# Layers 3 and 4 of a coupling network as pairs of 64-wide tiles, with the layers of successive blocks interleaved

## The chip, the cores and the metric

The kernel runs on one core of a Trainium2 chip. The metric is the device time of one execution in microseconds. Five engines work side by side: TensorE (PE), VectorE (DVE), ScalarE (ACT), GpSimd (POOL) and SyncE (SP), which issues the transfers.

## What is computed

```python
x = x + layernorm(attention(layernorm(x)))           # x: (8, 512, 256)
x = x + layernorm(ffn(layernorm(x)))

def coupling_net(h):                                  # 256 -> 256 -> 128 -> 64 -> 1
    h = gelu(h @ w1 + b1)
    h = gelu(h @ w2 + b2)
    h = gelu(h @ w3 + b3)
    return sigmoid(h @ w4 + b4)

def ffn(x):
    gf = global_net(x.mean(axis=1, keepdims=True))    # 256 -> 128 -> 64 -> 1
    out = x
    for _ in range(3):
        combined = 0.7 * gf + 0.3 * coupling_net(out)
        coupling = 0.1 + adaptive_range * (combined - 0.5) * 2.0
        out = out + coupling * twist(out)             # twist permutes and negates quarters
    return out
```

The attention is a segmented one with a memory carried from segment to segment. The change does not touch it.

## The kernel before, in words

The attention takes the first 1075 us or so and works in four steps (segments of 128 rows) for each of four pairs of sequences. Its very end overlaps the start of the feed-forward part: the last segment's rows are still to be turned (`turn_att`, L1157), projected (`project_out`, L1172), normalised and added (`y_stats`, `y_norm`, `residual`, `x2_stats`, `x2_norm`) and turned once more (`turn_rows`, L1044), and these steps are written by hand between the first feed-forward stages.

The feed-forward part holds the activations transposed in SBUF (`XT`, features on partitions, float32). The 8 x 512 rows are four blocks `bb` (one for each pair of sequences), and a block is two halves `j` of 512 columns. There are three cycles over the four blocks, so twelve **stages**, here numbered m = 0 to 11; the code before counts halves, n = 2m. The four stages of cycle 2 (m = 4 to 7) are a hardware loop, the others are written out. A stage is `layers(n, bb)`:

- `layer1` (L1278): four results per stage, each of two matmuls (256 = 2 x 128 rows), 128x512, into four PSUM banks; ACT applies gelu to each (L636).
- `layer2` (L1291): two results, each of two matmuls, into two banks; gelu (L644).
- `layers34`: for each half one matmul of w3 (L1298), which gives 64 output partitions, always partitions 0 to 63, and a gelu over 64 partitions (L649); then for each half one matmul of w4 (L1301), which contracts these 64 rows and gives the same sum on all 128 partitions, and a tanh (L658).
- `update` on DVE: two TENSOR_SCALARs make the coupling from the tanh (L961), then L966, L967 and L969 the products and the sum for the first 128 features; POOL subtracts for the other 128 (L456).

A float32 matmul is two records of PE in the trace, and each has a weight load before it.

Every engine runs its own instruction list in order and waits on semaphores. The order of the work is written out by hand, once for each engine. `net(half, layer)` is the small global network: half 0 (the first three pairs) in stage 0, half 1 (the last pair) in stage 3, where it waits for `seq_sums` (L849, L861) on DVE. `couple` turns its result into the base of the coupling.

In cycle 3 each block is finished after its stage. `back(t)` (L1262) transposes a tile of 128x512 back into a PSUM bank, four tiles for each block; `f_stats` (L976, L979) and `f_shift` (L984) on DVE with `f_dev` (L461, L463) on POOL give the layer norm's scale and shift; ACT normalises into SBUF (L674); POOL adds the residual (L468; DVE adds the last two tiles, L997); SP stores a block in eight transfers (L346). DVE and POOL have `finish(bb - 1)` ahead of `update` of stage 8 + bb. `back` of a block stands on PE in the stage after it, between layer 2 and layer 3:

```python
layer1(n, bb, half, last - NSEG if last else None)
layer2(n)
if last is not None:
    ...
    for t in range(last, last + NSEG):
        ...
        back(t)
layers34(n)
```

## Time and profile before

| | |
|---|---|
| time, median of 3 runs | 1298.55 us (1297.96 to 1299.42) |
| profiled execution, span | 1296.2 us |
| what lies around the span, against that median | 2.4 us |
| PE busy | 1091.5 us (84%) |
| DVE busy | 913.4 us (70%) |
| ACT busy | 596.7 us (46%) |
| POOL busy | 582.6 us (45%) |

The profiled execution has no time of its own among the three, only its span; its own time is taken as the span and the 2.4 us around it, and so stands level with the median. The span is cut into stretches below: the attention up to about 1075 us, the feed-forward stages from there to 1269 us, and the rest. A timeline row gives the start in us from the span's start, the length, the engine, the line, what is written and read, the shape and the number of records; in square brackets stands the idle time of the engine before it and who ended it. PEclk is the granted TensorE clock as a share of 2.4 GHz (1.00 is 2.4 GHz, 0.50 is 1.2 GHz).

### The profile page before, as it was taken

To read this page: it belongs to the slowest core of one execution; us is meant where nothing else is said; L and a number is where in the kernel's file an instruction comes from. 1 tells how busy PE (TensorE), PEld (TensorE's weight loads), DVE (VectorE), ACT (ScalarE), POOL (GpSimd) and SP (SyncE) were. 2 spreads that over 40 slices of the span, in tenths; PEclk is the share of its full clock that TensorE was granted. 3 is DMA by queue.
4 is the path that set the end of the run, shared out by engine and by line. 5 is a ranking of instruction groups with operands and counts; after the bars stand their busy time and mean duration, and the time that the engine had idled before them with its cause. 6 is when DMAs were issued, how large, how long until landed. Compare 5 with 4: busy or idle time off the path is not lost.

```text
span 1296.2 us, 20762 instructions
## 1 busy us (share of the span) xinstructions
PE 1091.5 (84%) x7108; PEld 764.7 (59%) x7172; DVE 913.4 (70%) x1668; ACT 596.7 (46%) x1255; POOL 582.6 (45%) x715
## 2 busy tenths in 40 slices
PE   3798889886989898878888888798989779999992
PEld 1476657564767575647676756576767665433431
DVE  4868686876686868657878786868686754444486
ACT  4344444544454444443535354445444543444463
POOL 2145454544454545434545454545454552222274
PEclk9899999988899999989999999989999888999996
DMA  5000000000000000000000000000000010300033
GB/s 159 20 9 9 10 9 11 8 14 6 10 9 9 9 9 10 10 10 10 9 9 9 9 10 9 9 9 9 9 1 9 1 28 1 138 0 0 1 65 65
DMA packets 14681, 24.00 MB, mean 19 GB/s; under 512 B 5104, under 2 KB 6896, under 8 KB 14064
## 3 DMA queue, kind: packets, MB, share of 16 engines
q1 hardware_dynamic: 14576, 22.63, 5.7%
q8 instruction: 62, 1.02, 0.3%
q14 instruction: 43, 0.35, 0.1%
HBM read 13.97 MB, written 8.65 MB: 17 GB/s over the span
## 4 chain that ended last, share of the span: by engine, by line
PE 41%; DVE 38%; issue 11%; ACT 6%; POOL 2%; DMA 1%; DVEq 1%; SPq 0%; POOLq 0%; ACTq 0%
DVE arena L769 10%; PE ps L1172 9%; PE ps L1067 8%; PE ps L1278 6%; DVE arena L867 3%; PE ps L1125 3%; DVE arena L788 3%; ACT arena L555 3%; PE ps L1291 3%; DVE arena L819 2%; PE ps L1112 2%; DVE arena L713 2%; DVE arena L801 2%; DVE arena L779 2%; DVE arena L782 2%
## 5 line engine op out<-in xcount | busy, mean ns | idle before, releaser
L1067 PE MATMUL ps<-arena 128*128 128x512 f16 x1152 | 270.8, 386 | 6.0 <-DVE arena L745 4.2
L555 ACT ACTIVATE arena<-ps,arena 128x128 f32<-128x128 f32 x512 | 140.7, 381 | 252.4 <-DVE arena L791 251.3
L769 DVE STREAM_TRANSPOSE arena<-ps 128x1024 f32<-128x1024 f32 x96 | 189.8, 1979 | 35.4 <-PE ps L1067 35.4
L1067 PEld LDWEIGHTS ps<-arena 128*128 128x128 f16 x1152 | 113.1, 100 | 129.4 <-issue 14.0
L402 POOL TENSOR_TENSOR arena<-arena 128x256 f32<-128x256 f32 x128 | 93.1, 728 | 153.3 <-DVE arena L801 153.3
L1125 PEld LDWEIGHTS ps<-arena 128*128 128x128 f32 x1024 | 135.7, 202 | 29.5 <-issue 21.2
L1125 PE MATMUL ps<-arena 128*128 128x65 f32 x1024 | 139.2, 281 | 16.2 <-DVE arena L801 15.0
L386 POOL TENSOR_TENSOR arena<-arena 128x512 f32<-128x512 f32 x64 | 81.2, 1268 | 135.4 <-ACT arena L548 135.2
L1112 PE MATMUL ps<-arena 128*128 128x128 f32 x512 | 84.5, 303 | 45.6 <-ACT arena L555 45.5
L1172 PE MATMUL ps<-arena 128*128 128x256 f32 x544 | 122.0, 382 | 0.3 <-ACT arena L567 0.3
L372 POOL TENSOR_TENSOR arena<-arena 128x2 f32<-128x2 f32 x50 | 9.8, 196 | 230.8 <-DVE arena L709 230.8
L1172 PEld LDWEIGHTS ps<-arena 128*128 128x128 f32 x544 | 102.0, 190 | 16.0 <-issue 0.8
L705 DVE BATCH_NORM_STATS2 arena<-arena 128x6 f32<-128x256 f32 x100 | 36.7, 409 | 100.1 <-ACT arena L573 85.0
L1145 PE MATMUL ps<-arena 128*128 128x130 f32 x384 | 69.3, 320 | 42.6 <-DVE arena L730 24.1
L1112 PEld LDWEIGHTS ps<-arena 128*128 128x128 f32 x512 | 63.1, 154 | 65.1 <-ACT arena L555 64.5
L404 POOL TENSOR_TENSOR arena<-arena 128x256 f32<-128x256 f32 x128 | 93.1, 728 | 10.0
L406 POOL TENSOR_TENSOR arena<-arena 128x256 f32<-128x256 f32 x128 | 93.1, 727 | 10.0
L801 DVE TENSOR_TENSOR arena<-ps,arena 128x512 f32<-128x512 f32 x128 | 88.5, 692 | 12.4
L788 DVE TENSOR_REDUCE arena<-ps 128x4 f32<-128x512 f32 x128 | 87.0, 680 | 13.1 <-PE ps L1101 12.7
L561 ACT ACTIVATE arena<-ps 128x1024 f32<-128x1024 f32 x64 | 65.7, 1026 | 65.9 <-PE ps L1112 65.9
L713 DVE TENSOR_SCALAR arena<-arena 128x256 f32<-128x256 f32 x100 | 68.7, 728 | 36.5 <-POOL arena L374 36.5
L1130 PE MATMUL ps<-arena 128*128 128x130 f32 x512 | 91.0, 303 | 0.0
(110 smaller groups left out, 1920.9 us busy)
## 6 DMA issues: line engine op xcount, KB each, us to landing
x_rows<-arena SPq DMA_DIRECT2D x17, 256.0 KB, 2.0
arena<-in_L_attn_x_dram SPq DMA_DIRECT2D x64, 64.0 KB
arena<-x_rows SPq DMA_DIRECT2D x4, 1024.0 KB, 7.9
out_dram<-arena SPq DMA_DIRECT2D x32, 128.0 KB, 2.9
arena<-in_L_attn_Wq_dram SPq DMA_DIRECT2D x1, 1024.0 KB, 12.3
arena<-in_L_attn_Wk_dram SPq DMA_DIRECT2D x1, 1024.0 KB, 14.4
arena<-in_L_attn_Wv_dram SPq DMA_DIRECT2D x1, 1024.0 KB, 17.4
arena<-in_L_attn_Wo_dram SPq DMA_DIRECT2D x1, 1024.0 KB, 13.0
```

The lines of the kernel that those rows point to most:

```text
L402: pool.tensor_tensor(mem, mem, dot, ALU.subtract).then_inc(mix, 1)
L404: pool.tensor_tensor(mem, mem, gt, ALU.mult).then_inc(mix, 1)
L406: pool.tensor_tensor(att[:, u * DK:(u + 4) * DK].rearrange("p (u e) -> p u e", u=4), mem, dot, ALU.add).then_inc(att_done, 1)
L555: last = act.activation(Pr[:, par, j, :], s_bank[:, par, j * P:(j + 1) * P], ACT.Exp, scale=SCALE, bias=shift[:, par, j:j + 1])
L713: last = dve.tensor_scalar(dst[:, w * D:(w + 1) * D], src[:, w * D:(w + 1) * D], mv[:, w, 0:1], rs[:, w:w + 1], ALU.subtract, ALU.mult)
L769: dve.transpose(dst[:, d0:d0 + 32, :], bank.rearrange("p w (d c) -> p d w c", c=C)).then_inc(x_free, 1)
L788: dve.tensor_reduce(negm[:, par, :], s_bank[:, par, :].rearrange("p (j i) -> p j i", j=GP), AX.X, ALU.max, negate=True).then_inc(m_done, 1)
L801: dve.tensor_tensor(AB[half], rd[:, :, :, 0:DK], rr.rearrange("p m (u a) -> p m u a", a=1).to_broadcast([P, 2, 4, DK]), ALU.mult).then_inc ...
L1067: last = pe.matmul(bank[:, w, :], xc[:, lx, k, w * P:(w + 1) * P], W16[lw][:, k, i, :], start=(n == 0), stop=(n == 5))
L1112: last = pe.transpose(s_bank[:, par, j * P:(j + 1) * P], Pr[:, par, j, :], identf)
L1125: pe.matmul(pm_bank[:, 0, u * DV1:(u + 1) * DV1], PT[:, par, j, :], v[:, GU * g + 2 * j + par, 0:DV1], start=True, stop=True)
L1172: last = pe.matmul(t_bank[b][:, w * D:(w + 1) * D], attT[:, w, j, :], Wo_sb[:, j, :], start=(j == 0), stop=(j == 7))
```

## The change

`layer3` writes its second half to partitions 64 to 127 of the same bank, so both halves share one bank and one gelu over 128 partitions, and one semaphore step instead of two. In the built program the second matmul carries the array position (0, 64) in tiles of 128x64. `layer4` contracts partitions 0 to 63 for the first half and 64 to 127 for the second (array positions (0, 0) and (64, 0), tiles of 64x128), into two different banks, with one semaphore step. w4 and b3 are loaded a second time onto the upper partitions (two transfers more), and `h3` is one buffer.

A stage m now runs layer 1 of its first half, layer 3 of stage m - 1, layer 1 of its second half, layer 4 of stage m - 1, layer 2. Layer 4 of stage 0 stands after `project_out`. On DVE and POOL `update` of stage 0 moves behind `y_norm` and `residual`. In cycle 3 the finishes move one place back in each list and `back` moves out of the stages: block 0 is transposed after stage 10, block 1 after stage 11, blocks 2 and 3 after the last layer 4. New banks are given to layers 3 and 4 and to `back`, with waits on them: layer 1 of stage 11 and layer 4 of stage 10 now wait for the normalised tiles of block 0.

```diff
-        l3_bank = [l1_bank[0], l1_bank[2]]
-        back_bank = [ps[:, b, :] for b in (1, 5, 2, 3)]
+        l3_bank = l2_bank[0]
+        y_job = t_job(PAIRS - 1, NSEG, "Y")
+        pair_bank = t_bank[y_job[0]]
+        solo_bank = t_bank[1 - y_job[0]]
+        back_banks = [(l1_bank[2], l1_bank[3], solo_bank, pair_bank)] * 2 + [
+            tuple(l1_bank), (l2_bank[0], l2_bank[1], solo_bank, pair_bank)]
         net_job = [t_job(PAIRS - 1, NSEG, j) for j in ("A1", "F")]
+
+        def back_bank(t):
+
+            return back_banks[t // NSEG][t % NSEG]
+
+        def l4_bank(m, j):
+
+            return (l2_bank[1], l2_bank[0] if isinstance(m, int) and m in (0, LAST_M) else pair_bank)[j]
...
-                        (w3, cw3), (w4[0:64], cw4), (g1, gw1.rearrange("(k p) n -> p k n", k=KT)), (g2, gw2),
+                        (w3, cw3), (w4[0:64], cw4), (w4[64:P], cw4), (g1, gw1.rearrange("(k p) n -> p k n", k=KT)), (g2, gw2),
                         (g3[0:64], gw3), (b1, cb1.rearrange("(m p) -> p m", m=2)), (b2, col(cb2)),
-                        (b3[0:64], col(cb3)), (b4, col(cb4).to_broadcast([P, 1])), (c1, col(gb1)),
+                        (b3[0:64], col(cb3)), (b3[64:P], col(cb3)), (b4, col(cb4).to_broadcast([P, 1])), (c1, col(gb1)),
...
-                update(0, 0)
                 y_dev(PAIRS - 1, NSEG)
                 residual(PAIRS - 1, NSEG)
+                update(0, 0)
                 x2_dev(PAIRS - 1, NSEG)
...
+                update(2 * CYCLE_M, 0)
+                update(2 * CYCLE_M + 1, 1)
+                finish(0)
+                update(2 * CYCLE_M + 2, 2)
+                finish(1)
+                finish(2)
+                finish(3, 2)
...
+                def stage(m, prev=None, half=None, last=None):
+
+                    if half is not None:
+                        net(half, 0)
+                    layer1(m, 0)
+                    if last is not None:
+                        normalise(last)
+                    if prev is not None:
+                        layer3(prev)
+                    if last is not None:
+                        normalise(last + 1)
+                    if half is not None:
+                        net(half, 1)
+                    layer1(m, 1)
+                    if half is not None:
+                        net(half, 2)
+                    if last is not None:
+                        normalise(last + 2)
+                        normalise(last + 3)
+                    if prev is not None:
+                        layer4(prev)
+                    layer2(m)
...
+                layer3(0)
+                take_y(y_job)
+                layer4(0)
+                stage(1)
                 take_f(t_job(PAIRS - 1, NSEG, "F"), NT - 1)
-                layers(4)
-                layers(6, 1)
+                stage(2, 1)
+                stage(3, 2, 1)
...
-                update(0, 0)
                 y_stats(PAIRS - 1, NSEG)
                 y_norm(PAIRS - 1, NSEG)
+                update(0, 0)
                 x2_stats(PAIRS - 1, NSEG)
                 x2_norm(PAIRS - 1, NSEG)
-                update(2, 1)
+                update(1, 1)
                 seq_sums(PAIRS - 1, NSEG)
-                update(4, 2)
+                update(2, 2)
                 couple(1)
-                update(6, 3)
+                update(3, 3)
...
+                update(2 * CYCLE_M, 0)
+                update(2 * CYCLE_M + 1, 1)
+                finish(0)
+                update(2 * CYCLE_M + 2, 2)
+                finish(1)
+                update(LAST_M, 3, True)
+                finish(2)
+                finish(3)
...
+                def back(bb):
+
+                    for t in range(bb * NSEG, (bb + 1) * NSEG):
+                        done = (2 * CYCLE_M + bb) * 2 + t % NSEG // 2 + 1
+                        pe.wait_ge(up_a, done)
+                        pe.wait_ge(up_b, done)
+                        if bb == 3 and t % NSEG < 2:
+                            pe.wait_ge(th_done, 2 * LAST_M + 2)
+                        elif bb < 2 and t % NSEG == 3:
+                            pe.wait_ge(th_done, 2 * (2 * CYCLE_M + bb + 1) + 2)
+                        if t >= NSEG:
+                            pe.wait_ge(fn_done, 2 * (t - NSEG + 1))
+                        for w in range(2):
+                            for k in range(KT):
+                                last = pe.transpose(back_bank(t)[:, w * D + k * P:w * D + (k + 1) * P],
+                                                    XT[:, k, (2 * t + w + 2) * P:(2 * t + w + 3) * P], identf)
+                        last.then_inc(f_full, 1)
...
+                    for c in range(2):
+                        if last is not None and j == 1:
+                            pe.wait_ge(fn_done, 2 * (last + c + 1))
...
+                        pe.wait_ge(l1_act, m * 4 + 2 * (j + 1))
+                        if isinstance(m, int) and m == 1:
+                            pe.wait_ge(th_done, 2)
+                        elif j == 1 and not (isinstance(m, int) and m == 0):
+                            pe.wait_ge(th_done, m * 2 - 1)
+                        for k in range(2):
+                            done = pe.matmul(l2_bank[j], w2[:, k, :], h1[j][:, k, :],
+                                             start=(k == 0), stop=(k == 1))
+                        done.then_inc(l2_full, 1)
+
+                def layer3(m):
+                    pe.wait_ge(l2_act, m * 2 + 2)
+                    for j in range(2):
+                        done = pe.matmul(l3_bank[64 * j:64 * j + 64], w3, h2[j], start=True, stop=True)
+                    done.then_inc(l3_full, 1)
+
+                def layer4(m, last=None):
+                    pe.wait_ge(l3_act, m + 1)
+                    if isinstance(m, int) and m == 1:
+                        pe.wait_ge(t_free[y_job[0]], y_job[1] + 1)
+                    if not (isinstance(m, int) and m == 0):
+                        pe.wait_ge(th_done, m * 2)
+                    if last is not None:
+                        pe.wait_ge(fn_done, 2 * (last + NSEG))
+                    for j in range(2):
+                        p = slice(64 * j, 64 * j + 64)
+                        done = pe.matmul(l4_bank(m, j), w4r[p], h3[p], start=True, stop=True)
+                    done.then_inc(l4_full, 1)
+
...
+                    layer1(m, bb, 0)
+                    if prev is not None:
+                        layer3(prev)
+                    if half is not None:
+                        net(half, 1)
+                    layer1(m, bb, 1, last)
                     if half is not None:
+                    if prev is not None:
+                        layer4(prev, last)
+                    layer2(m)
...
-                layers34(0)
-                project_out(t_job(PAIRS - 1, NSEG, "Y"), [t_job(PAIRS - 1, NSEG, a) for a in ("A2", "A3")])
-                layers(2, 1)
+                layer3(0)
+                project_out(y_job, [t_job(PAIRS - 1, NSEG, a) for a in ("A2", "A3")])
+                layer4(0)
+                stage(1, 1)
                 turn_rows(t_job(PAIRS - 1, NSEG, "F"), row, x2n_done, NT + 1)
-                layers(4, 2)
+                stage(2, 2, 1)
                 pe.wait_ge(xt_done, NT + 1)
-                layers(6, 3, 1)
+                stage(3, 3, 2, 1)
...
+                    m = 2 * CYCLE_M + bb
+                    stage(m, bb, m - 1, None, 0 if bb == PAIRS - 1 else None)
+                    if bb >= 2:
+                        back(bb - 2)
+                layer3(LAST_M)
+                layer4(LAST_M)
+                back(PAIRS - 2)
+                back(PAIRS - 1)
```

The update function's counts change from n to 2m and are the same otherwise. (L1320, L1333, L1340, L1353 and L1307 of the new file are layers 1, 2, 3, 4 and `back`; L993 to L1001 the update.)

**PE, the end of the program**, from layer 1 of stage 11. Before:

```order
L1278 MATMUL ps<-arena 128x512 x8
L1291 MATMUL ps<-arena 128x512 x4
L1262 MATMUL ps<-arena 128x128 x16
L1298 MATMUL ps<-arena 64x512 x2
L1301 MATMUL ps<-arena 128x512 x2
```

and in the change, where the first L1307 is block 0's `back`, after stage 10:

```order
L1307 MATMUL ps<-arena 128x128 x16
L1320 MATMUL ps<-arena 128x512 x4
L1340 MATMUL ps<-arena 64x512 x2
L1320 MATMUL ps<-arena 128x512 x4
L1353 MATMUL ps<-arena 128x512 x2
L1333 MATMUL ps<-arena 128x512 x4
L1307 MATMUL ps<-arena 128x128 x16
L1340 MATMUL ps<-arena 64x512 x2
L1353 MATMUL ps<-arena 128x512 x2
L1307 MATMUL ps<-arena 128x128 x32
```

Layers 3 and 4 of a stage moved into the stage behind it, and two blocks are left to be transposed at the very end, where one was.

**DVE, the start of the feed-forward part.** Before, the update of stage 0 and then the two normalisations:

```order
L961 TENSOR_SCALAR arena<-arena 128x16x16 x2
L966 TENSOR_TENSOR arena<-arena 128x512
L967 TENSOR_TENSOR arena<-arena 128x512
L969 TENSOR_TENSOR arena<-arena 128x512
L705 BN_STATS arena<-arena 128x6 x2
L707 MEMSET arena 128x1
L709 BN_AGGR arena<-arena 128x2 x2
L713 TENSOR_SCALAR arena<-arena 128x256 x2
L705 BN_STATS arena<-arena 128x6 x2
```

and in the change:

```order
L737 BN_STATS arena<-arena 128x6 x2
L739 MEMSET arena 128x1
L741 BN_AGGR arena<-arena 128x2 x2
L745 TENSOR_SCALAR arena<-arena 128x256 x2
L993 TENSOR_SCALAR arena<-arena 128x16x16 x2
L998 TENSOR_TENSOR arena<-arena 128x512
L999 TENSOR_TENSOR arena<-arena 128x512
L1001 TENSOR_TENSOR arena<-arena 128x512
```

The update (its second half follows with the same four rows) now stands between the first and the second normalisation of the last rows.

## Rows read from the trace of the kernel before

**Rows 1.** Page, part 1: busy time, share of the span, instructions of each engine.
```profile
PE 1091.5 (84%) x7108; PEld 764.7 (59%) x7172; DVE 913.4 (70%) x1668; ACT 596.7 (46%) x1255; POOL 582.6 (45%) x715
```
**Rows 2.** Busy time by stretch: window, length, engines, PEclk, DMA share, GB/s.
```profile
1203.28:1217.55 14.27, 14.27 (x34) 5.48 (x33) 6.34 (x11) 6.87 (x11) 3.23 (x2) 1.00 0.00 0
1276.00:1284.00 8.00, 3.88 (x16) 3.14 (x16) 7.67 (x24) 1.60 (x4) 2.28 (x6) 0.50 0.53 120
```
**Rows 3.** Timeline of PE, one steady stage: start, length, line, shape, records.
```profile
1203.28 7.13 PE L1278 MATMUL ps<-arena 128*128 128x512 f32 x16
1210.25 3.60 PE L1291 MATMUL ps<-arena 128*128 128x512 f32 x8
1213.78 1.93 PE L1298 MATMUL ps<-arena 128*64 128x512 f32 x4
1215.64 1.98 PE L1301 MATMUL ps<-arena 64*128 64x512 f32 x4
```
**Rows 4.** Timeline of PE in the attention: the score matmuls in two row halves.
```profile
1005.23 0.84 PE L1101 MATMUL ps<-arena 64*128 64x128 f16 x24
```
**Rows 5.** Timeline of PE, the first four stages of the feed-forward part.
```profile
1090.96 1.93 PE L1298 MATMUL ps<-arena 128*64 128x512 f32 x4
1094.73 7.17 PE L1172 MATMUL ps<-arena 128*128 128x256 f32 x32
...
1115.91 0.66 PE L1044 MATMUL ps<-arena 128*128 128x128 f32 x4
1116.40 7.03 PE L1278 MATMUL ps<-arena 128*128 128x512 f32 x16
...
1130.57 0.61 PE L1249 MATMUL ps<-arena 128*128 128x2 f32 x4
...
1146.20 7.13 PE L1278 MATMUL ps<-arena 128*128 x16
```
**Rows 6.** Timeline of DVE over the same stages.
```profile
1094.78 0.74 DVE L961 TENSOR_SCALAR arena<-arena 128x256 f32<-128x256 f32 x2 [8.67 <-ACT arena L658]
...
1102.58 0.75 DVE L705 BATCH_NORM_STATS2 arena<-arena 128x6 f32<-128x256 f32 x2 [1.35 <-ACT arena L573]
...
1108.96 0.73 DVE L713 TENSOR_SCALAR arena<-arena 128x256 f32<-128x256 f32 x2 [1.09 <-POOL arena L374]
1115.88 0.74 DVE L961 TENSOR_SCALAR arena<-arena 128x256 f32<-128x256 f32 x2 [6.19 <-ACT arena L658]
...
1122.97 0.51 DVE L861 TENSOR_TENSOR arena<-arena 128x4 f32<-128x4 f32 x1
```
**Rows 7.** Timeline of POOL: the residual add between the two normalisations.
```profile
1105.52 1.27 POOL L417 TENSOR_TENSOR arena<-arena 128x512 f32<-128x512 f32 x1 [0.85 <-DVE arena L713]
```
**Rows 8.** Timeline of PE: one pair's transposes back.
```profile
1245.65 1.94 PE L1262 MATMUL ps<-arena 128*128 128x128 f32 x16 [1.52 <-issue]
```
**Rows 9.** Timeline of DVE from the first finish to the last add.
```profile
1228.59 0.76 DVE L976 BATCH_NORM_STATS2 arena<-ps 128x6 f32<-128x256 f32 x2 [4.62 <-PE ps L1262]
...
1235.06 2.71 DVE L961 TENSOR_SCALAR arena<-arena 128x256 f32<-128x256 f32 x2
...
1264.07 0.76 DVE L976 BATCH_NORM_STATS2 arena<-ps 128x6 f32<-128x256 f32 x2 [1.89 <-PE ps L1262]
...
1280.07 0.76 DVE L976 BATCH_NORM_STATS2 arena<-ps 128x6 f32<-128x256 f32 x2
...
1287.72 1.18 DVE L997 TENSOR_TENSOR arena<-arena 128x512 f32<-128x512 f32 x1 [0.49 <-ACT arena L674]
```
**Rows 10.** Timeline of POOL: adds of one pair of tile rows; last deviation.
```profile
1269.35 5.02 POOL L468 TENSOR_TENSOR arena<-arena 128x512 f32<-128x512 f32 x4
...
1281.19 0.20 POOL L461 TENSOR_TENSOR arena<-arena 128x2 f32<-128x2 f32 x1 [6.82 <-DVE arena L979]
```
**Rows 11.** Timeline of ACT: two tiles normalised, four instructions.
```profile
1267.83 1.91 ACT L674 ACTIVATE arena<-ps,arena 128x256 f32<-128x256 f32 x4
```
**Rows 12.** Timeline of SP: the 32 output transfers, four groups of eight.
```profile
1238.92 54.47 SPq L346 DMA_DIRECT2D out_dram<-arena  x32
```

More of the change, by code:

```diff
@@ L156, in infini_block_kernel @@
         h1 = [alloc(2 * NB).rearrange("p (m n) -> p m n", m=2) for _ in range(2)]
[L157 removed]
+        h2, th, cs, PA, PB = ([alloc(NB) for _ in range(2)] for _ in range(5))
+        h3 = alloc(NB)
         fn = [alloc(TILE) for _ in range(4)]
@@ L628, in net @@
                         act.activation(gh[2][:, cols], z, ACT.Tanh, bias=c3, scale=0.5).then_inc(gc_act, 1)
-                def layer1(n, half=None):
-                    for j in range(2):
-                        if half is not None:
-                            net(half, j)
-                        for m in range(2):
-                            act.wait_ge(l1_full, n * 2 + (2 * j + m + 1))
-                            act.activation(h1[j][:, m, :], l1_bank[2 * j + m], ACT.Gelu,
-                                           bias=b1[:, m:m + 1]).then_inc(l1_act, 1)
-                    if half is not None:
-                        net(half, 2)
@@ L1282, in layer1, with stage @@
+                def stage(m, bb, prev=None, half=None, last=None):
+                    if half is not None:
+                        net(half, 0)
+                    layer1(m, bb, 0)
+                    if prev is not None:
+                        layer3(prev)
+                    if half is not None:
+                        net(half, 1)
+                    layer1(m, bb, 1, last)
                     if half is not None:
                         net(half, 2)
-                def layer2(n):
-                    for j in range(2):
-                        pe.wait_ge(l1_act, n * 2 + 2 * (j + 1))
-                        if not (isinstance(n, int) and n == 0):
-                            pe.wait_ge(th_done, n + j - 1)
-                        for k in range(2):
-                            last = pe.matmul(l2_bank[j], w2[:, k, :], h1[j][:, k, :],
-                                             start=(k == 0), stop=(k == 1))
-                        last.then_inc(l2_full, 1)
@@ L1295, in layers34 @@
-                def layers34(n):
-                    for j in range(2):
-                        pe.wait_ge(l2_act, n + (j + 1))
-                        pe.matmul(l3_bank[j][0:64], w3, h2[j], start=True, stop=True).then_inc(l3_full, 1)
-                    for j in range(2):
-                        pe.wait_ge(l3_act, n + (j + 1))
-                        pe.matmul(l2_bank[j], w4r[0:64], h3[j][0:64], start=True,
-                                  stop=True).then_inc(l4_full, 1)
-                def layers(n, bb, half=None, last=None):
-                    layer1(n, bb, half, last - NSEG if last else None)
-                    layer2(n)
-                    if last is not None:
-                        pe.wait_ge(up_a, n)
-                        pe.wait_ge(up_b, n)
-                        for t in range(last, last + NSEG):
-                            if t >= 4:
-                                pe.wait_ge(fn_done, 2 * (t - 3))
-                            back(t)
-                    layers34(n)
```

144 lines of the change are left out of this document (59 added, 85 removed).

## The prediction

> **What bounds the kernel now.** I read the page's busy shares first, then the stretches, then the timelines of PE, DVE, ACT and POOL from the start of the feed-forward part. PE leads with 84% [rows 1], but what a change in one stage is worth has to be read there. In a steady stage PE is busy in all 14.27 us, while DVE has 6.3, ACT 6.9 and POOL 3.2 [rows 2]: the middle is PE's alone. The tail is not. From the first finish at 1228.59 to the last add at 1288.90 [rows 9] DVE's list is one chain: a finish takes 6.5 us (1228.59 to 1235.06), and a finish with the update behind it 16.0 (1264.07 to 1280.07), because the four adds of POOL, 5.0 us [rows 10], hold up DVE's instructions behind the finish: the pair L961 takes 2.71 us instead of 0.74 [rows 6, 9]. PE idles there 1.5 us per stage [rows 8]. So three places count: the pairs on PE, and what the new order does at either end, where DVE sets the pace.
>
> **A steady stage.** Layer 1 has 16 records, layer 2 has 8, layers 3 and 4 have 4 each [rows 3]: 32, about 0.43 us apart (512 columns at two cycles each and 2.4 GHz are 0.427; I take 0.4285). 32 x 0.4285 = 13.71; the missing 0.56 of 14.27 I put to the three changes of array shape (128x128 to 128x64 to 64x128 and back), 0.19 each; layer 3's 1.86 us from start to start hold 4 x 0.43 and 0.15 of it [rows 3].
> The change makes four changes of shape (0.76) and leaves 24 full records (10.28). Open is what a pair of half-array matmuls takes; no float32 pair is in the trace. It lies between 0.86 (both side by side) and 1.72 (no overlap, as now). The nearest row is the attention's scores: 24 fp16 records of 128 columns in two row halves take 0.84 us [rows 4]. One after the other they would need 24 x 0.054 = 1.29 (0.4285 is two cycles for each of 512 columns, these take one for each of 128), so two do run side by side. But there the halves alternate in program order. Here each matmul is two records, and the order is first half, first half, second half, second half. If PE starts records strictly in order, the third can only start together with the second, which waits for the first: three spaces of 0.43, 1.29 us a pair. I take 1.29 for both pairs. The stage is 10.28 + 0.76 + 2 x 1.29 = **13.62**, 0.65 less than 14.27; 12.76 at the lower end, 14.48 at the upper.
> The Trainium skill, "TensorE: Matmul & The Clock Gate", Part 3, gives the span of a pack as one matmul's duration plus some 4 ns per tile; by that the pair takes 0.86 and the first rival below holds. The same part says that matmuls never pass each other in start or end, which is the reading taken here; the trace's scores agree with both.
> ACT loses 0.7 us of gelu per stage and the gelus' waits lie behind 3.4 us of layer 1; neither is on PE's path, so both cost and gain nothing. The two small transfers more end long before 1075 us; nothing.
>
> **The start.** Layer 3 of stage 0 starts at 1090.96 as now [rows 5] and takes 1.48 with its change of shape; `project_out` follows at 1092.4 and takes 7.0 (7.17 in its row [rows 5], whose modelled end reaches 0.15 into the next), so it ends at 1099.4. Layer 4 ends at 1100.9, stage 1 (layers 1 and 2 alone) at 1111.4.
> DVE's first statistics start 0.8 after the projection (1102.58 [rows 6]), now 1100.2. From there to the second normalisation's end at 1109.69 are 7.1 us, with 1.4 of POOL's residual add in the middle [rows 6, 7]: 2.9 for each. The first ends at 1103.1. Behind it stands the update: 6.4 us (1115.88 to 1122.97, less 0.7 for the reduction of `seq_sums`), plus 0.9 because POOL's residual add, 1.27 [rows 7], runs beside its first pair: until 1110.5. The second normalisation takes another 2.9 (statistics, POOL, L713 [rows 6]), to 1113.4. Only then can PE turn the last rows: it waits **2.0 us** where it waited for nothing. Stage 2 starts at 1113.9, against 1116.40 [rows 5], but stage 1's layers 3 and 4 are still owed.
> Layer 4 of stage 1 ends 9.8 into stage 2 (3.43 + 1.48 + 3.43 + 1.48). DVE's update starts 0.9 behind a layer 4 (at 1094.78, and it needs the first half alone, whose matmul was through 0.86 before layer 4's end at 1094.73 [rows 5, 6]), and `seq_sums` ends 7.6 after its start (1115.88 to 1123.48 [rows 6]): 1113.9 + 9.8 + 0.9 + 7.6 = 1132.3. The global net opens stage 3 and waits for it, while PE is through with stage 2 at 1127.5. A **stall of 4.8 us** takes the place of none. Stage 3 with the net takes 15.6 (1130.57 to 1146.20 [rows 5]) less 0.65. The idle may cost clock as well: after DVE had held PE for 7.8 us the granted clock stood at 0.50 [rows 2]. Bounds: nothing, or layer 1's first 3.4 us at half speed, 3.4; I take 1.3, since this idle is shorter. Stage 4 then starts at 1132.3 + 15.0 + 1.3 = **1148.6**, 2.4 behind before's 1146.20. Stage 10 starts six stages later, at 1148.6 + 81.7 = **1230.3**.
>
> **The tail,** counted from stage 10's start. Layer 4 of stage 9 ends at 9.8, update 9 runs 10.8 to 17.2, finish 0 to 23.9 (its tiles are turned at 13.6 to 15.5, 1.84 a block [rows 8]). Stage 11's layer 1 ends about 24.3. Layer 4 of stage 10 waits for all four tiles of block 0 to be normalised, and ACT has two of these behind its last gelu: 25.2 + 1.9 [rows 11] = 27.1. So PE idles 2.8, and update 10 starts only at 29.6 and ends at 36.0; DVE has nothing to do between 23.9 and 29.6. From here DVE runs on without a pause, since layer 4 of stage 11 ends at 38.0: finish 1 and update 11 take 16.1, to 52.1, finish 2 6.5, to 58.6. POOL's order then delays finish 3: its deviations stand behind four adds that start 5.3 after finish 2 did and take 5.0 [rows 10], so until 62.5; in the trace the first deviation (1281.19) is 7.7 before the last add's end: 70.2. The last eight transfers take 7.3 more (1288.9 to 1296.2; SP's row begins with the first and ends near 1293.4 [rows 12]). **Tail 77.5.** Before, update 9 started at 1235.06 with finish 0 done [rows 9]. Now update 9 starts at 1241.1, finish 0 comes on top, and DVE waits 5.7 in between.
>
> **Sum.** 1230.3 + 77.5 = 1307.8, and 2.4 around the span: **1310.2 us**, 11.7 above the median. A difference of 0.2% (2.6 us) is about what a measurement of this kernel can tell from no change.
>
> **The rivals.**
> - *Pairs fully side by side* (0.86). For it: the scores' overlap [rows 4]. Against it: records there alternate. The stall in stage 3 then ends at 1131.0, stage 4 starts at 1146.4, stage 10 at 1222.9, the tail is 76.5 (the wait on ACT hides most of the gain): 1299.4, so 1301.8 us.
> - *No overlap of float32 halves*: stage 14.48, one change of shape more than now. Stage 4 at 1150.7, stage 10 at 1237.6, tail 79: 1319 us. Nothing in the trace excludes it, as no column pair and no float32 pair is there.
> - *Faster*: the pairs run side by side and the breaks of 0.19 around them vanish too, since half of the array is free while the other ends. The stage is 10.28 + 1.72 = 12.0, stage 4 starts at 1145.1, stage 10 at 1217.1, the tail is 76: 1295.5 us. It decides from a stage below some 12.4 us. Against it: before has each break at the start of a half-array layer as well [rows 3]. An overestimate of DVE's waits at the two ends by half would do the same for the first rival.
>
> **How the numbers follow.** Forecast 0.56, fully side by side 0.20, no overlap 0.10, faster 0.14. Side by side lands at +0.25%, so half of its chance counts as no change: slower 0.56 + 0.10 + 0.10 = 0.76, same 0.10, faster 0.14. The range takes in the faster cases down to 1295.5 and the forecast with the clock's bound and up to 0.2 us more per pair (1316), and leaves out the no-overlap case and misses of mine. The forecast's own range is 1305 to 1315.
>
> **What would show it.** Stage length in the loop 13.6 (12.8 or 14.5 for the rivals), and the starts of the four records of a pair: 0, 0.43, 0.43, 0.86. PE idle 2 us before the last L1079 and 4.8 us before the net in stage 3. DVE idle some 5.7 us before update 10, PE about 2.8 before stage 10's layer 4. Finish 3 with POOL's adds between its deviations. The forecast is wrong if stage 10 starts before 1222, or if the tail from there is shorter than 73.

## The result, and the profile after

| | before | change |
|---|---|---|
| time, median | 1298.26 us (1295.55 to 1299.42, 4 runs) | 1304.70 us (1303.94 to 1305.81, 4 runs) |
| ratio | | 1.0045 [1.0028, 1.0063] |
| span of the profiled execution | 1296.2 us | 1302.3 us |
| first record of the feed-forward part (global net) | 1075.22 us | 1078.03 us |
| from there to the end | 220.94 us | 224.26 us |

The kernel became slower by 6.4 us, where the forecast said 11.7. The two profiles differ by 6.1 us, but 2.8 of these lie in the attention, which the change does not touch: over the twelve traces of this case the feed-forward part began between 1072.7 and 1081.0 us. In what follows times are therefore counted from the first record of the global net, and the length from there to the end is called **F**. The change's own doing is F: 220.94 to 224.26, +3.3 us. It splits into three:

| stretch | before | change | |
|---|---|---|---|
| start of F to stage 4 | 70.98 | 71.88 | +0.9 |
| stage 4 to stage 10 | 87.36 | 76.58 | -10.8 |
| stage 10 to the end | 62.64 | 75.81 | +13.2 |

The page's first part, of the change. PE is 14 us less busy and the kernel is not faster:

```profile
PE 1077.8 (83%) x7108; PEld 756.9 (58%) x7172; DVE 908.3 (70%) x1668; ACT 590.8 (45%) x1243; POOL 581.6 (45%) x715
```

The stretches of the change (columns as in [rows 2]): the first 4 us of work behind the stall in stage 3, one steady stage, the six stages 4 to 9, and the tail from stage 10:

```profile
1134.00:1138.00 4.00, 4.00 (x8) 2.15 (x9) 0.00 (x0) 0.27 (x1) 0.00 (x0) 0.50 0.02 4
...
1200.96:1213.73 12.77, 12.77 (x34) 4.90 (x33) 6.40 (x11) 6.09 (x9) 3.23 (x2) 1.00 0.00 0
...
1149.91:1226.49 76.58, 76.58 (x194) 29.36 (x192) 39.20 (x63) 36.57 (x54) 19.88 (x13) 1.00 0.00 0
...
1226.49:1302.30 75.81, 39.59 (x137) 19.07 (x135) 48.40 (x120) 30.54 (x54) 41.91 (x52) 0.76 0.26 56
```

The same two last stretches of before:

```profile
1146.20:1233.56 87.36, 87.36 (x209) 34.73 (x208) 41.95 (x79) 41.61 (x62) 23.09 (x20) 1.00 0.00 0
1233.56:1296.20 62.64, 36.37 (x113) 17.70 (x112) 46.57 (x95) 27.79 (x52) 36.03 (x43) 0.81 0.32 67
```

In the middle PE is busy without a gap in both kernels, so the 10.8 us are PE's alone. In the tail PE has half of its time free, and DVE is the busiest.

The timeline of PE in the change, first the start of the feed-forward part, then a steady stage, then the tail:

```profile
1078.03 0.86 PE L1284 MATMUL ps<-arena 128*128 128x6 f32 x4
...
1109.76 3.60 PE L1333 MATMUL ps<-arena 128*128 128x512 f32 x8
...
1115.57 0.66 PE L1079 MATMUL ps<-arena 128*128 128x128 f32 x4 [2.22 <-DVE arena L745]
1116.06 3.60 PE L1320 MATMUL ps<-arena 128*128 128x512 f32 x8
...
1125.29 3.70 PE L1333 MATMUL ps<-arena 128*128 128x512 f32 x8
...
1133.81 0.99 PE L1284 MATMUL ps<-arena 128*128 128x2 f32 x4 [4.82 <-DVE arena L893]
1134.66 5.81 PE L1320 MATMUL ps<-arena 128*128 128x512 f32 x8
...
1200.96 3.60 PE L1320 MATMUL ps<-arena 128*128 128x512 f32 x8
1204.49 1.08 PE L1340 MATMUL ps<-arena 128*64 128x512 f32 x4
1205.50 3.70 PE L1320 MATMUL ps<-arena 128*128 128x512 f32 x8
1209.13 1.13 PE L1353 MATMUL ps<-arena 64*128 64x512 f32 x4
1210.19 3.70 PE L1333 MATMUL ps<-arena 128*128 128x512 f32 x8
1213.73 3.60 PE L1320 MATMUL ps<-arena 128*128 128x512 f32 x8
...
1246.45 3.67 PE L1320 MATMUL ps<-arena 128*128 128x512 f32 x8 [0.84 <-ACT arena L676]
...
1252.82 1.13 PE L1353 MATMUL ps<-arena 64*128 64x512 f32 x4 [2.70 <-ACT arena L676]
```

From start to start, layer 3 of a pair takes 1.01 us (1204.49 to 1205.50) and layer 4 takes 1.06 (1209.13 to 1210.19); one after the other they were 1.86 and 1.91 [rows 3]. The single records show how. Program order is first half, first half, second half, second half; the four records of layer 3 start at 1204.489, 1204.496, 1204.969 and 1204.976, those of layer 4 at 1209.129, .136, .662 and .669. The starts come in couples 7 ns apart and not at 0, 0.43, 0.43, 0.86 as the forecast had it. The trace does not name the half of a record; that each couple is one record of each half follows from before, where four records on the same half took 1.86 us from start to start, over 0.43 each [rows 3]. All twelve pairs of layer 3 in this trace have this pattern.

The timeline of DVE in the change: update 1, which starts inside stage 2, the end of `seq_sums` behind it, and the tail (update 9, finish 0, update 10, update 11, finish 2, finish 3, the last add):

```profile
1126.13 0.73 DVE L993 TENSOR_SCALAR arena<-arena 128x256 f32<-128x256 f32 x2 [10.62 <-ACT arena L667]
...
1133.21 0.50 DVE L893 TENSOR_TENSOR arena<-arena 128x4 f32<-128x4 f32 x1
...
1236.56 0.73 DVE L993 TENSOR_SCALAR arena<-arena 128x256 f32<-128x256 f32 x2 [6.32 <-ACT arena L667]
...
1242.92 0.76 DVE L1008 BATCH_NORM_STATS2 arena<-ps 128x6 f32<-128x256 f32 x2
...
1254.71 0.74 DVE L993 TENSOR_SCALAR arena<-arena 128x256 f32<-128x256 f32 x2 [5.20 <-ACT arena L667]
...
1267.61 2.71 DVE L993 TENSOR_SCALAR arena<-arena 128x256 f32<-128x256 f32 x2
...
1277.13 0.76 DVE L1008 BATCH_NORM_STATS2 arena<-ps 128x6 f32<-128x256 f32 x2
...
1283.61 0.75 DVE L1008 BATCH_NORM_STATS2 arena<-ps 128x6 f32<-128x256 f32 x2
...
1288.30 0.16 DVE L1016 SCALAR_TENSOR_TENSOR arena<-arena 128x2 f32<-128x2 f32 x1 [2.73 <-POOL arena L479]
...
1293.82 1.18 DVE L1029 TENSOR_TENSOR arena<-arena 128x512 f32<-128x512 f32 x1 [0.49 <-ACT arena L676]
```

Before, finish 0 was through when update 9 began, 1.5 us after stage 10's start [rows 9]; now update 9 begins 10.1 us after it (1236.56 less 1226.49) and finish 0 comes on top. That is the interleaving's doing: the tanh of stage 9 is computed inside stage 10. DVE then idles 5.20 us before update 10, in part because layer 4 of stage 10 had to wait 2.70 us for ACT's normalised tiles (the last experiment below takes 0.92 off the one and 0.94 off the other). It idles 2.73 us more in finish 3 for POOL, whose four adds stand before the deviation that is wanted:

```profile
1282.40 4.93 POOL L484 TENSOR_TENSOR arena<-arena 128x512 f32<-128x512 f32 x4
1287.29 0.20 POOL L477 TENSOR_TENSOR arena<-arena 128x2 f32<-128x2 f32 x1
```

### The profile page after: what moved, and what is told of

Its sections match the earlier page's. It is cut to its first block, busy times and chain, and to the rows that moved or that the text cites. A ratio compares the mean times of both kernels' runs of the same rounds, so it can differ in the third digit from the quotient of the medians.

```text
span 1302.3 us, 20762 instructions
## 1 busy us (share of the span) xinstructions
PE 1077.8 (83%) x7108; PEld 756.9 (58%) x7172; DVE 908.3 (70%) x1668; ACT 590.8 (45%) x1243; POOL 581.6 (45%) x715
## 3 DMA queue, kind: packets, MB, share of 16 engines
q8 instruction: 63, 1.03, 0.3%
## 4 chain that ended last, share of the span: by engine, by line
PE 41%; DVE 37%; issue 10%; ACT 7%; POOL 2%; DMA 1%; DVEq 1%; SPq 0%; POOLq 0%; ACTq 0%
DVE arena L801 10%; PE ps L1207 9%; PE ps L1102 8%; PE ps L1320 6%; PE ps L1160 3%; DVE arena L899 3%; DVE arena L820 3%; ACT arena L572 3%; PE ps L1333 2%; DVE arena L745 2%; DVE arena L851 2%; PE ps L1147 2%; DVE arena L811 2%; DVE arena L833 2%; DVE arena L814 2%
## 5 line engine op out<-in xcount | busy, mean ns | idle before, releaser
L1180 PE MATMUL ps<-arena 128*128 128x130 f32 x384 | 66.6, 309 | 44.4 <-DVE arena L762 24.2
L1320 PE MATMUL ps<-arena 128*128 128x512 f32 (+1 forms) x192 | 90.7, 617 | 0.8 <-ACT arena L676 0.8
## 6 DMA issues: line engine op xcount, KB each, us to landing
arena<-in_L_attn_Wv_dram SPq DMA_DIRECT2D x1, 1024.0 KB, 17.2
```

Source lines behind the costliest of these rows:

```text
L1320: done = pe.matmul(l1_bank[2 * j + c], w1[:, k, c * P:(c + 1) * P], XT[:, k, bass.ds((bb * 4 + (2 * j + 1)) * 2 * P, NB)], start=(k == 0), ...
```

## The experiments

The theory after the result: a pair runs side by side whatever its program order, and the interleaved order delays DVE's list at both ends, by a stall of 4.8 us in stage 3 and by waits in the tail. The rivals are told at each run. F, counted as above, is the sharper measure for kernels that differ by little; the table puts it beside the ratio. A ratio is against runs of before that were timed beside it; their medians were 1298.26, 1300.93, 1298.68 and 1299.79 us. A kernel that was timed once has no ratio.

| run | F, us | F less that of before, us | ratio to before |
|---|---|---|---|
| before, again | 220.72 | -0.2 | |
| change | 224.26 | +3.3 | 1.0045 [1.0028, 1.0063] |
| seq_first | 217.71 | -3.2 | 0.9972 [0.9955, 0.999] |
| one_half | 243.79 | +22.9 | 1.016 [1.0113, 1.0207] |
| quarters | 224.46 | +3.5 | 1.0015 [0.9996, 1.0034] |
| norm_first | 222.47 | +1.5 | |
| pool_tail | 225.47 | +4.5 | |
| combined | 215.41 | -5.5 | 0.997 [0.9956, 0.9983] |
| pairs_alone | 221.88 | +0.9 | 1.001 [0.9995, 1.0024] |
| mended | 212.30 | -8.6 | 0.9927 [0.9905, 0.9949] |
| in_four | 228.86 | +7.9 | |

**The scatter first.** Before once more, on the chip of the first experiments:

> The kernel before, for its trace alone. The changed kernel's profiled execution reached the first feed-forward matmul 2.8 us later than that of before, though the attention's program is the same. Theory: this is scatter of the loads and of the clock, so this trace lies off the first one by up to 3 us there, while from that matmul to the end it takes 220.9 us within 0.3. Rival: the change delays the attention; then this trace reaches it at 1075.2 within 0.5 us.

Its only run took 1303.21 us, 5 more than the median beside the change, and the first record of the net came at 1080.68 instead of 1075.22; F is 220.72 against 220.94:

```profile
1080.68 0.86 PE L1249 MATMUL ps<-arena 128*128 128x6 f32 x4
```

The first record was expected to lie off by up to 3 us and lies off by 5.5; F was expected within 0.3 and is. So a single time says nothing about 3 us here, and F does. F has a smaller scatter of its own. Its first layer 1, which no edit touches, took between 4.68 us (the change) and 5.80 us (the last kernel below) over the twelve traces, with 0.77 and 0.62 of the clock granted in it, so a difference of F under some 1 us has to be looked up in the trace.

**The pair.** Without the overlap: both halves on the same part of the array, so that one follows the other (the second half's layer 3 overwrites the first's and layer 4 reads partitions 0 to 63 for both, so the values computed differ):

```diff
-done = pe.matmul(l3_bank[64 * j:64 * j + 64], w3, h2[j], start=True, stop=True)
+done = pe.matmul(l3_bank[0:64], w3, h2[j], start=True, stop=True)
...
-p = slice(64 * j, 64 * j + 64)
+p = slice(0, 64)
```

> The changed kernel with both matmuls of layer 3 written to partitions 0 to 63 and both of layer 4 contracted over partitions 0 to 63; the interleaving, the waits and the instruction counts stay. It computes layers 3 and 4 of the second half from the first half's place, so the values are others. Theory: in the changed kernel the two halves run side by side (a pair takes 0.86 us), so here each pair takes 0.86 us more: the stage goes from 12.77 to 14.48 us, and with some 8 such stages ahead of the tail the time is about 14 us longer, 1318 us. Rival: the pairs gain little and the shorter stage comes from the interleaving, which hides waits of PE: stage below 13.2, under 1308 us.

Measured: the stage is 14.47 us, 1.70 more than 12.77. The stretch, and PE's two rows, of this kernel:

```profile
1212.59:1227.06 14.47, 14.47 (x34) 5.53 (x33) 6.40 (x11) 6.08 (x9) 3.22 (x2) 1.00 0.00 0
```

```profile
1216.12 1.93 PE L1340 MATMUL ps<-arena 128*64 128x512 f32 x4
...
1221.61 1.98 PE L1353 MATMUL ps<-arena 64*128 64x512 f32 x4
```

The place in the array alone makes 0.85 us a pair, one whole matmul of the two. The theory had the stage at 14.48. Up to stage 10 this kernel needs 15.2 us more than the change, where some 14 were expected, and another 4.3 in the tail, where its clock fell to 0.50 during layers 4 and 2 as well. It also shows what the interleaving gives PE by itself: with layers one after the other in the new order, 14.47 is no better than the old 14.27.

The second run cuts each matmul of layer 3 into two of 256 columns, in the order A, A, B, B, and those of layer 4 likewise, but alternating:

```diff
+for q in range(2):
+    c = slice(256 * q, 256 * q + 256)
-    done = pe.matmul(l3_bank[64 * j:64 * j + 64], w3, h2[j], start=True, stop=True)
+    done = pe.matmul(l3_bank[64 * j:64 * j + 64, c], w3, h2[j][:, c], start=True, stop=True)
```

> The changed kernel with every matmul of layers 3 and 4 cut into two of 256 columns. In layer 3 the order is first half, first half, second half, second half; in layer 4 it alternates between the halves. Theory A (matmuls start in program order, but the two records of one float32 matmul don't hold up a neighbour in the other half): layer 3 takes 0.43 us more than now (from its start to the next layer's 1.44 instead of 1.01), layer 4 stays at 1.06 us; the time is some 3 to 4 us longer, 1308 us. Theory B (the halves of the array run independently of each other, each in its own order): both stay within 0.1 us of 1.01 and 1.06, and the time is the same within 1.5 us.

Both took what the uncut pairs take (PE's rows of this kernel):

```profile
1203.90 1.09 PE L1342 MATMUL ps<-arena 128*64 128x256 f32 x8
1204.93 3.70 PE L1320 MATMUL ps<-arena 128*128 128x512 f32 x8
1208.56 1.13 PE L1358 MATMUL ps<-arena 64*128 64x256 f32 x8
```

In layer 3 the first records of A and B start at 1203.905 and 1203.919, though three more records of A stand between them in program order. That is theory B of the two: the order makes no difference at this length. As the kernel does on PE what the change does, its ratio, 1.0015 [0.9996, 1.0034], is a second measurement of the change's cost, from other executions; F agrees within 0.2 us. Taken together the two put the change's price nearer to the 3.3 us of F, 0.25%, than to 0.45%.

Does the order ever matter? Layer 3 cut in four of 128 columns, all of A first, then all of B:

```diff
+for q in range(4):
+    c = slice(128 * q, 128 * q + 128)
-    done = pe.matmul(l3_bank[64 * j:64 * j + 64], w3, h2[j], start=True, stop=True)
+    done = pe.matmul(l3_bank[64 * j:64 * j + 64, c], w3, h2[j][:, c], start=True, stop=True)
```

> The changed kernel with each matmul of layer 3 cut into four of 128 columns, all of the first half ahead of all of the second: eight records stand between the second half's first one and its turn. Theory: the halves of the array run independently, each in its own order, so layer 3 still takes 1.0 to 1.15 us from its start to the next layer's. Rival: PE sees only a few records ahead (in the cut into two, four records were passed), the second half begins late, and layer 3 takes 1.25 us or more.

It does (PE's rows of this kernel):

```profile
1205.96 1.58 PE L1342 MATMUL ps<-arena 128*64 128x128 f32 x16
1207.47 3.70 PE L1320 MATMUL ps<-arena 128*128 128x512 f32 x8
```

The pair takes 1.51 us instead of 1.03. A's first record starts at 1205.962, B's first only at 1206.455, beside A's fifth at 1206.449, and all twelve pairs of this trace show the same. The rival held. In both runs B's first record starts when exactly three records of A are still waiting: in the cut into two right behind A's first of four, here behind A's fifth of eight. The two records of a half in the change stay below that; eight do not. That the order does it, and not the shorter records, is argued from this: the cut into four with the halves alternating was not run.

**The pairs without the new order.** The pairs put into before's order (layers 3 and 4 of a stage at its end, layer 3 in layer 1's bank, one gelu):

```diff
-        l3_bank = [l1_bank[0], l1_bank[2]]
+        l3_bank = l1_bank[0]
...
+                    act.wait_ge(l3_full, n + 2)
+                    act.activation(h3, l3_bank, ACT.Gelu, bias=b3).then_inc(l3_act, 2)
...
-                        pe.wait_ge(l3_act, n + (j + 1))
+                    pe.wait_ge(l3_act, n + 2)
```

> The kernel before, with the pairs of layers 3 and 4 (one bank, one gelu over 128 partitions, array positions in both halves), but in its old order: a stage's own layers 1, 2, 3, 4. Theory: the pairs take 1.0 us each as in the change, but PE now waits for the gelu of layer 2's second half and then for the gelu of layer 3, about 0.95 us each: the stage takes 14.4 to 14.5 us, against 14.27 before and 12.77 in the change, and the time is within 2.5 us of before. Rival: the waits are hidden or short, the stage is under 13.5 us and the time 7 us shorter than before, without any interleaving.

The stage is 14.33 us, just under the 14.4 to 14.5 expected, and PE is now busy in only 12.70 of them; the stretch, then PE's rows:

```profile
1201.21:1215.54 14.33, 12.70 (x34) 4.97 (x32) 6.30 (x10) 6.08 (x9) 3.23 (x2) 1.00 0.00 0
```

```profile
1212.56 1.08 PE L1297 MATMUL ps<-arena 128*64 128x512 f32 x4 [0.78 <-ACT arena L645]
...
1214.48 1.13 PE L1302 MATMUL ps<-arena 64*128 64x512 f32 x4 [0.85 <-ACT arena L649]
```

The pair's saving is there and turns into two waits for gelu, 0.78 and 0.85 us. Pairs alone 14.33, new order alone 14.47, both together 12.77: neither part gives anything without the other. Before, each half's matmul covered the other half's gelu. Of the 0.9 us that F is longer than before's, 0.8 lie in the first layer 1 (5.67 us against 4.85), which is scatter.

**The stall in stage 3.** `seq_sums`, which needs nothing of stage 1, moved ahead of update 1 on DVE:

```diff
-update(1, 1)
 seq_sums(PAIRS - 1, NSEG)
+update(1, 1)
```

> The changed kernel with one step moved on DVE: the sums for the last pair's global net (L881, L893) stand ahead of the update of stage 1 instead of behind it. In the changed kernel PE was idle for 4.82 us before the net of stage 3, and layer 1 behind it ran 5.81 us instead of 3.60, the clock having fallen. Theory: this idle is a pure wait for DVE's order, so it goes, and the clock stays at 1.00: stage 3 begins 4.8 us earlier and runs about 2.6 us shorter, 7.4 us in all, about 1297.3 us. Rival: the wait only moves (the net needs ACT or the last rows, which come late in any order), and under 2 us are won, 1303 us or more.

The net follows layer 2 of stage 2 with no wait, and the clock stays at 2.4 GHz (PE's rows of this kernel):

```profile
1126.00 3.70 PE L1333 MATMUL ps<-arena 128*128 128x512 f32 x8
1129.54 0.50 PE L1284 MATMUL ps<-arena 128*128 128x2 f32 x4
1129.90 3.68 PE L1320 MATMUL ps<-arena 128*128 128x512 f32 x8
```

Stage 4 starts 7.41 us earlier than in the change: 4.82 of wait and some 2.6 of clock. That second part is read directly. Behind the wait the granted clock is 0.50 (the first row of stretches above), layer 1 takes 5.81 us instead of 3.60 and the net 0.99 instead of 0.50. Stage 10 gains the same 7.41, but F only 6.55. Behind PE's wait for layer 4 of stage 10 the clock fell in this run, and that layer 4 takes 2.08 us instead of the 1.13 of the change, which waited as long (2.70 us) and kept its clock. The stretch of this kernel, then PE's row in it:

```profile
1245.00:1250.00 5.00, 4.08 (x8) 1.62 (x9) 1.21 (x3) 2.04 (x4) 2.42 (x2) 0.66 0.32 60
```

```profile
1245.91 2.08 PE L1353 MATMUL ps<-arena 64*128 64x512 f32 x4 [2.69 <-ACT arena L676]
```

One moved line turns the change from slower into slightly faster than before, 0.9972 [0.9955, 0.999].

**The wait before the last rows.** `x2_stats` and `x2_norm` (DVE) and `x2_dev` (POOL) ahead of update 0:

```diff
-update(0, 0)
 x2_stats(PAIRS - 1, NSEG)
 x2_norm(PAIRS - 1, NSEG)
+update(0, 0)
...
-update(0, 0)
 x2_dev(PAIRS - 1, NSEG)
+update(0, 0)
```

> The changed kernel with the update of stage 0 moved behind the second normalisation of the last rows, on DVE and POOL. Theory: PE's idle of 2.22 us before the last rows' transposes (L1079) goes, and everything up to stage 10 comes 2.2 us earlier, counted from the first feed-forward matmul; the wait of 4.8 us before stage 3 stays. From that matmul to the end 222 us instead of 224.3. Rival: the update of stage 0, now late, holds up the update of stage 1 and the wait before stage 3 grows by as much; nothing is won.

The wait of 2.22 us before L1079 is gone and that of 4.82 before the net is not (PE's rows):

```profile
1116.93 0.60 PE L1079 MATMUL ps<-arena 128*128 128x128 f32 x4
...
1135.12 0.99 PE L1284 MATMUL ps<-arena 128*128 128x2 f32 x4 [4.82 <-DVE arena L893]
```

F is 1.8 us shorter, and the first layer 1 happened to be 0.8 us longer than in the change's trace, so the edit's own gain is nearer to 2.6. The second wait stays as it was because DVE there waits for the tanh of stage 1, which moves with PE: the two waits add.

**POOL's order in the tail.** The deviations of block 2 and the first of block 3 taken ahead of the adds:

```diff
-finish(2)
-finish(3, 2)
+for s in range(NSEG):
+    f_dev(2 * NSEG + s)
+for s in range(NSEG):
+    add(2 * NSEG + s)
+    f_dev(3 * NSEG + s)
+add(3 * NSEG)
+add(3 * NSEG + 1)
```

> The changed kernel with POOL's last part in another order: the deviations of block 3 alternate with the adds of block 2 instead of standing behind all four of them. Theory: DVE's idle of 2.73 us in the last finish (before L1016) falls to under 0.7 us and the end comes 2 to 2.7 us earlier: 221.6 to 222.3 us from the first feed-forward matmul to the end, against 224.3. Rival: the adds, now late, delay the normalisation of block 3 (it needs their buffers) and block 2's stores, and the end moves less than 1 us.

A miss: F is 225.47, 1.2 us longer than the change's. DVE's rows show where most of it comes from:

```profile
1282.34 1.21 DVE L1021 SCALAR_TENSOR_TENSOR arena<-arena 128x2 f32<-128x2 f32 x1 [0.16 <-POOL arena L479]
...
1288.81 1.21 DVE L1021 SCALAR_TENSOR_TENSOR arena<-arena 128x2 f32<-128x2 f32 x1 [0.95 <-POOL arena L479]
...
1291.11 1.18 DVE L1034 TENSOR_TENSOR arena<-arena 128x512 f32<-128x512 f32 x1 [0.49 <-ACT arena L681]
```

The wait of 2.73 us is gone, but now all four shifts of block 3 start beside an add of POOL and take 1.21 us, where three of the change's took 0.13 to 0.16 and only the last 1.21. That is 3.2 us more work for 2.7 us of wait, and finish 3 takes 9.80 us instead of 9.12; another 0.4 lie between the last add's end and the end of the span (7.7 us against 7.3). In the change the statistics of block 3 stand beside the adds, and they take 0.75 us as without them (1283.61 above, inside the adds of 1282.40 to 1287.33). So POOL's adds are not free by standing elsewhere: in these traces they cost DVE nothing beside statistics that read PSUM, or while it waits.

**All three.**

> The changed kernel with all three orders mended: the sums for the net ahead of the update of stage 1, the update of stage 0 behind the second normalisation, and POOL's deviations of block 3 between the adds of block 2. Theory: the gains add up, 7.4 + 2.2 + 2.5 = 12 us off the changed kernel: 212 to 213 us from the first feed-forward matmul to the end, against 224.3 for the change and 220.9 before, so about 8 us or 0.6% faster than before. Rival: PE, coming earlier, meets DVE later (update of stages 0 and 1 back to back), and 3 us or more are given back.

F is 215.41, 8.9 less than the change's, where the first two edits alone gave 8.3 (6.5 and 1.8), each with scatter against it. Without the clock's 0.9 in the tail of the one and the 0.8 in the first layer 1 of the other they are worth some 10, and POOL's part takes about 1 off again, as it did alone. The timed runs agree that it beats before, 0.997 [0.9956, 0.9983], but it does not reach the 212 to 213 expected.

**A mended version.** The first two edits; on POOL only the deviations of blocks 2 and 3, DVE taking these adds between its statistics and shifts; and on ACT in stage 11 the third and fourth tile of block 0 normalised each straight behind a gelu of layer 1, so that layer 4 waits less:

```diff
 POOL:
-finish(2)
-finish(3, 2)
+for t in range(2 * NSEG, 4 * NSEG):
+    f_dev(t)
 ACT, stage with a block to finish:
-layer1(m, 1)
+for k in range(2):
+    act.wait_ge(l1_full, m * 4 + (2 + k + 1))
+    act.activation(h1[1][:, k, :], l1_bank[2 + k], ACT.Gelu, bias=b1[:, k:k + 1]).then_inc(l1_act, 1)
+    normalise(last + 2 + k)
 DVE, end:
+f_stats(8); f_stats(9); f_shift(8); f_stats(10); f_shift(9); f_stats(11); f_shift(10)
+add(8); f_shift(11); add(9); add(10); f_stats(12); add(11); f_stats(13); f_shift(12)
...
```

> The changed kernel with the two mended orders of the start (the sums for the net ahead of the update of stage 1, the update of stage 0 behind the second normalisation) and another tail: POOL's order as in the change but without adds for blocks 2 and 3; DVE makes these eight adds itself, three of them before the statistics of block 3; ACT normalises the third and fourth tile of block 0 right behind each gelu of layer 1. Theory: the start gives 9.6 us (7.4 + 2.2), the earlier normalisation lets layer 4 of stage 10 start 0.9 us earlier, and the tail loses POOL's wait (2.73 us) and two adds at half speed, 3 to 4 us: 210 to 211.5 us from the first feed-forward matmul to the end, against 224.3 for the change and 220.9 before; some 10 us, 0.75%, faster than before. Rival: the adds lengthen DVE's chain by what they save on POOL; then it is 214 us or more.

F is 212.30 and the ratio 0.9927 [0.9905, 0.9949]: faster than both kernels, though not the 210 to 211.5 expected; 1.1 us of it is its slow first layer 1. PE's wait before layer 4 of stage 10 fell from 2.70 to 1.78 us, DVE's before update 10 from 5.20 to 4.26, and the one in finish 3 is 0.85 instead of 2.73. PE's row, then DVE's:

```profile
1241.07 1.13 PE L1377 MATMUL ps<-arena 64*128 64x512 f32 x4 [1.78 <-ACT arena L676]
```

```profile
1242.96 0.74 DVE L997 TENSOR_SCALAR arena<-arena 128x256 f32<-128x256 f32 x2 [4.26 <-ACT arena L667]
...
1279.19 0.16 DVE L1020 SCALAR_TENSOR_TENSOR arena<-arena 128x2 f32<-128x2 f32 x1 [0.85 <-POOL arena L479]
```

From stage 10 to the end it takes 72.8 us against the change's 75.8, still 10 more than before's 62.6. Which of the three edits of the tail brought how much was not taken apart.

## Why the prediction was right in direction and too high in size

Direction and mechanism held: the middle gains, the start stalls, the tail gives more back. The time, 1304.7, is inside the range and 5.5 below the forecast. That is closer than the forecast deserves: F was forecast at 232.6 (1307.8 less 1075.2) and is 224.26, 8.3 too high, and the attention, which came 2.8 us later in the change's profiled execution than in before's, hides part of it. The 8.3 are 1.5 in the start, 5.1 in stages 4 to 9 and 1.7 in the tail.

- **The failing step is the price of the pair**, taken at three spaces of 0.43: "If PE starts records strictly in order, the third can only start together with the second". It starts 7 ns behind the first. A pair with its change of shape costs 1.01 and 1.06 us instead of the 1.48 taken, a stage 12.77 instead of 13.62. Through stages 4 to 9 alone that is 5.1 us (76.58 against 81.7). Of the signs named beforehand, the stage's length and the records' starts showed it; the two that were to call the forecast wrong did not (stage 10 starts at 1226.49, not before 1222, and the tail is over 73), so they were set too wide. The Trainium skill, "TensorE: Matmul & The Clock Gate", Part 3, has both rules that were weighed: its span of one matmul plus 4 ns per tile gives 0.86 a pair and is what the trace shows; its statement that matmuls never pass each other in start does not hold here for two halves of the array.
- **The first rival, pairs fully side by side, was the right one** and its stage was exact, 12.76 (12.77). That its sum is too, F 224.2 (224.26), is partly luck: its start is 0.7 too short (71.2, measured 71.88) and its tail 0.7 too long (76.5, measured 75.8). Its chance, 0.20, was too low. The scores' 24 records [rows 4] had shown the overlap; that they alternate in the program was taken as a condition, and nothing in the trace had said so.
- **The waits** were read off the lists of DVE, ACT and POOL nearly to size: before the last rows 2.0 (2.22), before the net 4.8 (4.82), before layer 4 of stage 10 2.8 (2.70, and 0.84 before a layer 1, which was not foreseen), before update 10 5.7 (5.20). POOL's adds ahead of finish 3's deviations are there too, and DVE waits 2.73 for them.
- **The clock** behind the stall costs 2.6 instead of 1.3. The reason given, that this idle was shorter than the one seen, did not hold; the bound of 3.4 did. The start as a whole is 71.88 long; the forecast said 73.4.
- **The tail** was put at 77.5 and is 75.8. 0.5 of this is a slip in the sum: by its own terms layer 1 of stage 11 ends at 23.8 (15.5 + 3.43 + 1.48 + 3.43) and not at 24.3, and what stands behind it comes 0.5 earlier. Finish 0 likewise ends at 23.7 (17.2 + 6.5) and not at 23.9, which changes nothing behind it.
- **ACT at nothing**: stands for the middle, where 0.7 us of gelu less changed nothing on PE.

What stays open: that a half passes three waiting records and no more was read from two kernels of one shape, without the alternating control; why the same wait of PE was followed by a lower clock in one execution and not in another; and the scatter of the attention, some 8 us between executions.

## What to carry to other kernels

Two matmuls on different halves of the array run at the price of one even when the program writes them one after the other, as long as each is only a few records (two and four were, eight were not); but merging the halves takes away the work that covered each half's activation, so the pair pays only if other matmuls are put between the layers. Interleaving moves every consumer of the last layer a stage later: ask at both ends of the loop what stands behind that consumer on its engine, and move what does not need it (here `seq_sums`) ahead. Where two executions differ by more than the effect, count from the last point that the change does not touch.

## What was not expected of the hardware

- Records of one half of the array start ahead of up to three waiting records of the other half: B's first starts 7 ns after A's first with two records per half, 14 ns with four, and with eight only beside A's fifth (0.493 us after A's first), when three of A are left.
- A change of array shape around a pair costs 0.15 to 0.20 us (1.01 and 1.06 less 0.86), the same as around the two single matmuls of before (1.86 and 1.91 less 1.72). The free half brought nothing here while the other ended, as the rival named faster supposed.
- An idle of 4.8 us of PE was followed by a granted clock of 0.50 and cost 2.6 us on top; one of 2.2 us before L1079 was followed by full-speed rows (3.60 us for eight records). The length of the idle does not decide alone: the same 2.7 us before layer 4 of stage 10 were followed by full speed in the change and by 0.50 in `seq_first`, where layer 4 took 2.08 us for 1.13.
- While POOL adds, the DVE pair L993 of update 11, which reads and writes SBUF, takes 2.71 instead of 0.73 us and a shift 1.21 instead of 0.16; statistics that read PSUM take 0.75 as without it (1283.61).
